# Layer norm of the next batch applied by VectorE instead of GpSimd, in a fused attention and feed-forward kernel

## The reference

```
def _layernorm(x, axis=-1, eps=1e-05):
    m = jnp.mean(x, axis=axis, keepdims=True)
    v = jnp.var(x, axis=axis, keepdims=True)
    return (x - m) / jnp.sqrt(v + eps)
...
    x = L0_attn_x
    xn = _layernorm(x, axis=-1)
    s = _L0_attn_ref(xn, L0_attn_W_attn, L0_attn_b_attn, L0_attn_W_proj, L0_attn_b_proj)
    g = _silu(_L0_ffn_ref(xn, L0_ffn_w_gate, L0_ffn_w_up, L0_ffn_w_down))
    x = x + s * g
    return x
```

## Time and profile before

| | |
|---|---|
| median of 3 runs | 1255.55 us (1254.56 to 1260.43) |
| profiled execution, its span | 1257.5 us |
| PE busy | 1197.4 us, 95% |
| DVE busy | 1013.0 us, 81% |
| ACT busy | 935.2 us, 74% |
| POOL busy | 693.3 us, 55% |
| granted TensorE clock, mean | 0.990 |
| one steady batch | 146.20 us |

### The profile page before, as it was taken

How to read it: one execution, slowest core, us unless ns; L and a number is a source line. 1 busy time by engine, 2 the same in 40 slices (tenths; PEclk the granted TensorE clock), 3 DMA queues, 4 the chain that set the end, 5 groups by cost and what they waited for, 6 DMA issues and landing times.

```text
span 1257.5 us, 29932 instructions
## 1 busy us (share of the span) xinstructions
PE 1197.4 (95%) x11324; PEld 558.3 (44%) x11324; DVE 1013.0 (81%) x2098; ACT 935.2 (74%) x1736; POOL 693.3 (55%) x863
## 2 busy tenths in 40 slices
PE   3889999999999999999999999999999999999986
PEld 2334444545345443544445453454445444454433
DVE  6678988888888888888888888888888888878732
ACT  4447777787877878778777878778787787778774
POOL 4527544395535937177453946369371874446472
PEclk9879999999999999999999999999999999999999
DMA  6140020401222120400204011221204002120101
GB/s 170 47 136 2 2 86 19 119 19 60 53 72 74 35 88 32 119 19 27 85 31 115 20 63 48 86 66 30 91 28 119 19 27 86 39 73 29 42 2 51
DMA packets 56004, 73.23 MB, mean 58 GB/s; under 512 B 8398, under 2 KB 34452, under 8 KB 55860
## 3 DMA queue, kind: packets, MB, share of 16 engines
q1 hardware_dynamic: 55848, 71.30, 18.9%
q10 hardware_dynamic: 12, 0.01, 0.0%
HBM read 44.96 MB, written 25.17 MB: 56 GB/s over the span
## 4 chain that ended last, share of the span: by engine, by line
PE 74%; POOL 10%; DVE 6%; issue 4%; ACT 4%; SPq 1%; DMA 1%; POOLq 0%; DVEq 0%; ACTq 0%
PE ring L854 31%; PE acc L845 17%; PE st L781 11%; PE ring L809 8%; PE ring L927 2%; DVE mx_a L1218 2%; POOL hf L1542 2%; PE ring L824 2%; ACT pexp L1055 2%; POOL hT L1551 1%; PE ring L864 1%; POOL xn L535 1%; PE ring L963 1%; POOL pexp L1512 1%; PE ring L942 1%
## 5 line engine op out<-in xcount | busy, mean ns | idle before, releaser
L1055 ACT ACTIVATE pexp<-st 128x512 f32<-128x512 f32 x1152 | 623.8, 598 | 124.0 <-PE st L781 123.3
L1218 DVE TENSOR_REDUCE mx_a<-ring 128x1 f32<-128x512 f32 (+2 forms) x960 | 536.8, 611 | 50.9 <-PE ring L809 26.0
L1512 POOL TENSOR_SCALAR_AFFINE_SELECT pexp<-pexp 128x512 f32<-128x512 f32 x256 | 158.4, 638 | 412.9 <-ACT pexp L1055 412.9
L845 PE MATMUL acc<-pexp,v_pad 128*17 128x512 f32 (+3 forms) x3072 | 303.7, 490 | 5.8 <-POOL pexp L1512 4.5
L809 PE MATMUL ring<-k_st,q_st 56*128 56x512 f16 (+4 forms) x1536 | 231.4, 326 | 13.3 <-POOL k_st L1641 3.4
L781 PE MATMUL st<-q_st,k_st 58*128 58x512 f16 (+3 forms) x1536 | 231.9, 331 | 6.1 <-ACT pexp L1055 3.4
L1218 DVE TENSOR_REDUCE mx_b<-ring 128x1 f32<-128x384 f32 (+2 forms) x448 | 210.4, 528 | 25.5 <-PE ring L824 24.7
L781 PEld LDWEIGHTS st<-q_st,k_st 58*128 58x128 f16 x1536 | 61.3, 93 | 265.2 <-ACT pexp L1055 173.4
L1542 POOL TENSOR_TENSOR hf<-ga,ups 128x512 f32<-128x512 f32 x96 | 122.4, 1275 | 42.0 <-issue 41.5
L845 PEld LDWEIGHTS acc<-pexp,v_pad 128*17 128x17 f32 x3072 | 61.9, 96 | 129.1 <-issue 105.7
L1551 POOL TENSOR_TENSOR hT<-hf,hT 128x512 f16<-128x512 f32 x96 | 111.4, 1161 | 3.4
(11 more groups left out here) (152 smaller groups left out, 1536.2 us busy)
## 6 DMA issues: line engine op xcount, KB each, us to landing
parts_scratch<-parts SPq DMA_DIRECT2D x32, 512.0 KB, 2.8
q_st<-parts_scratch SPq DMA_DIRECT2D x186, 64.0 KB, 2.2
k_st<-parts_scratch SPq DMA_DIRECT2D x186, 64.0 KB, 2.2
xo<-in_x SPq DMA_DIRECT2D x32, 256.0 KB, 2.9
out<-xo SPq DMA_DIRECT2D x32, 256.0 KB, 2.2
xn<-in_x SPq DMA_DIRECT2D x7, 1024.0 KB, 6.1
q_st<-mT SPq DMA_DIRECT2D x126, 4.0 KB
xn<-in_x SPq DMA_DIRECT2D x2, 512.0 KB, 6.2
```

The source lines that it names most:

```text
L845: mm = nc.tensor.matmul(acc[32 * j:32 * j + D + 1, CH - w:CH], v_pad[:, kb, GH * g + j, :], pexp[:, GH * (m % NSET) + j, at:at + w], start ...
L1055: nc.scalar.activation(pexp[:, GH * (n % NSET) + j, :], st[:, (GH * n + j) % NST, :], ACT.Exp, scale=1.0 / (QK_SCALE * np.sqrt(D))).then_i ...
L1218: top_ = nc.vector.reduce_max(dst, src, AX.X)
L1512: nc.gpsimd.affine_select(out=t, in_=t, compare_op=ALU.is_ge, fill=0.0, base=0, pattern=[[0, GH], [1, P]], channel_multiplier=-1).then_inc ...
```

## The change

LNA moves from GpSimd's list to VectorE's, with the same lag of one half slot and in the same slots. VectorE does it behind the maxima (and, in a half that has them, `split_maxima`) of the second half of slots 8 and 11 to 15, in the same order of tiles. The wait for the finished root, the pause (`stand`) and the instruction are the same. All else stays: the statistics on VectorE, the root on GpSimd, `xn_ready`, TX.

```
 LAG = {
...
-    "vector": {"TX": 0, "QK": 0, "UPG": 0, "DN": 0, "FT": 0, "YT": 0, "LNS": 1, "BP": 0},
-    "gpsimd": {"LNR": 0, "LNA": 1, "XC": 1, "UPU": 2, "HI": 3, "LO": 4, "FP": 2, "FP_G": 3, "FP_X": 4},
+    "vector": {"TX": 0, "QK": 0, "UPG": 0, "DN": 0, "FT": 0, "YT": 0, "LNS": 1, "BP": 0, "LNA": 1},
+    "gpsimd": {"LNR": 0, "XC": 1, "UPU": 2, "HI": 3, "LO": 4, "FP": 2, "FP_G": 3, "FP_X": 4},
...
                 if t[0] == "LNS":
                     return stats(kind, i, t[1])
+                if t[0] == "LNA":
+
+                    dve.wait_ge(ln_chain, LN_EACH * (ln_number(kind, i) + 1))
+                    stand(dve, dve_stand)
+                    return normalise(nc.vector, t[1])
...
                 if t[0] == "LNR":
                     rstd_steps(nc.gpsimd, kind, i, pool_stand)
-                if t[0] == "LNA":
-
-                    pool.wait_ge(ln_chain, LN_EACH * (ln_number(kind, i) + 1))
-                    stand(pool, pool_stand)
-                    normalise(nc.gpsimd, t[1])
```

## The result

| | before | after |
|---|---|---|
| median of 4 runs | 1257.32 us | 1285.97 us (1284.54 to 1287.27) |
| ratio | | 1.023, 95% interval 1.0205 to 1.0255 |
| profiled span | 1257.5 us | 1285.5 us |
| period of a batch, from the issues of the loads of x | 146.2 us | 150.1 us |

The change costs 2.3%, 28 us of span, 4 us a batch on average over seven. The prediction was 1.7% slower, 1276.5 us, in a range from 1254 to 1297. Executions of one kernel differ by some 5 us (the four of before run from 1254.56 to 1260.43), so that a median of few can move by 2 us: it was 1255.55 with three of them.

What follows compares the result with a forecast made beforehand. TensorE, busy 144.87 of 146.20 us a batch, was taken as the bound. Slot losses 1.63 + 0.35 + 0.97 = 2.95, say 3.0 us a batch, 21 us in seven, gave 1276.5 us, range 1254 to 1297.

Steps and rivals of the forecast that it cites:

- the ring: Four banks that VectorE's work frees and TensorE fills next; real slack at 409.89 taken as 0.15 us.
- The wait of 0.67 us: TensorE waits for GpSimd's causal mask at 417.43, once a batch; removing it wins 4.7 us at the most.
- The price of a step: Single step on VectorE 0.62 us, partly held by GpSimd; pair 2.45 at slot 8, 1.5 at slot 15.
- the one row at 1162.55: VectorE's small step on the maxima, a 0.19 us instruction, took 1.21 us, held by a GpSimd tensor_tensor.
- Slot 8: Two steps make VectorE 2.45 us late and TensorE 2.30; without the 0.67 wait, net loss 1.63 us a batch.
- Slot 15: Pair taken as 1.5 us, less idle 0.28 and slack 0.25: loss 0.97 us a batch.
- The uncounted term: VectorE's small steps on the maxima at 431 can be held too, up to 1.2 us each; not counted.
- Slots 11 to 15: Single steps before slot 15's pair: slot 12 loses 0.35 us, slot 11 nothing, slots 13 and 14 nothing or 0.2.
- No hold: Rival: VectorE pays only 0.29 to 0.41 us a step, 1255 to 1258 us; chance 0.16.
- Held to the full: Rival: every step pays 1.57 us, 8.2 us a batch, 1313 us; chance 0.11 for beyond 1297.

Runs made afterwards that it cites:

- relief_ts: relief with GpSimd's five two-input instructions replaced by the tensor_scalar form of its layer norm step; ratio 0.9963 to the kernel before, -4.6 us.
- split2: Kernel before, with GpSimd's two slot 8 steps moved to slots 12 and 14, and those of slots 11 and 13 to VectorE; ratio 0.9993, -0.9 us.
- dve_imm: Changed kernel with constants 0 and 1 in place of mean and root in VectorE's steps; ratio 1.0101 to the kernel before, +12.7 us.
- relief: Kernel before with GpSimd's eight layer norm steps each cut to one column, nothing on VectorE; ratio 1.0036, +4.5 us.
- dve_tiny: Changed kernel with VectorE's layer norm steps cut to one column; ratio 1.0035 to the kernel before, +4.4 us.
- after_ts: Changed kernel with GpSimd's five two-input instructions replaced by the tensor_scalar form of the layer norm step; ratio 1.0009 to the kernel before, +1.1 us.
- singles: Kernel before with only the four steps of slots 11 to 14 on VectorE, slots 8 and 15 left on GpSimd; ratio 1.0031, +3.9 us.

## Why the prediction was right, and where its sizes were off

- **What bounds the kernel.** Right. TensorE is full, and the ring between VectorE and TensorE is tight, but not as tight as read. At the second matmul of slot 9's maxima TensorE is 1.57 us late (409.89, now 419.28, less 7.82), behind a pair of steps that took 2.08. So the slack there was 0.5 us, not 0.15: the row of four maxima from 406.93 is 2.71 us long, where two take 1.29 and four without a break 2.5, so some 0.2 us of idle time of VectorE are hidden in it. I had 2.30 behind a pair of 2.45.
- **What GpSimd gives back.** The wait of 0.67 us is gone in the changed kernel, as forecast, under a larger loss in the same slot. That it is worth 4.7 us by itself fits relief_ts (-4.6), with the reserve above, and split2's steady batches.
- **The price of a step.** The direction was right, by the one row at 1162.55. Its parts were off. The undisturbed step takes 0.40 us, not the 0.29 of the row on b_pr: that row has constants as operands, and dve_imm shows that this is the difference. A held step does not pay its own time after the hold, as I had added it: it ends 0.15 us after GpSimd's instruction. And I counted products and casts only, where masks hold too. The mean in the kernel is 0.797, where I had (2.45 + 4 x 0.62 + 1.5) / 8 = 0.80. The singles are near (0.58 in the steady batch); the pairs are off in opposite directions (2.08 for 2.45, 2.19 for 1.5), so that the equality is luck.
- **Slot 8:** 0.84 us net for 1.63. The pair took 2.08 us, not 2.45: the second step did not come behind the cast with its full time, but ended 0.15 us after it. The rest of the miss is the slack, 0.5 for 0.15.
- **Slot 15:** 2.08 us for 0.97. This is the mis-sized term. I took 1.5 us for the pair, a middle between two bounds, since I couldn't read GpSimd's phase; it took 2.19, which is 0.69 of the miss. The other 0.42 is the slack of 0.53 that I took off: 0.11 was left, since the delays of the slots before had used up VectorE's idle stretch. The pair met two output instructions of 1.27 us one after the other:

```profile
443.16 1.27 POOL L1562 TENSOR_TENSOR so<-so,b_pr 128x512 f32<-128x512 f32 x1
...
443.73 2.19 DVE L535 TENSOR_SCALAR xn<-xn,lnv,rstd 128x256 f32<-128x256 f32 x2
444.50 1.26 POOL L1568 TENSOR_TENSOR so<-so,g 128x512 f32<-128x512 f32 x1
```

- **The uncounted term.** Slots 11 to 15 cost 0.99 us for 0.35: 0.13 where I had the 0.35, and 0.86 behind the steps on the maxima. These were named in the prediction with their price, up to 1.2 us each, and left at nothing: one of 1.23 us and one of 0.49 in a steady batch. The same term turns GpSimd's relief into a loss in relief and dve_tiny, which I hadn't foreseen.
- **The sum.** 0.84 + 0.99 + 2.08 = 3.91 for 2.95. The pair of slot 15 was 1.11 too small, the slots between 0.64 too small, slot 8 0.79 too large: net 0.96 us a batch, 6.7 in seven, of the 7.0 by which the span (1285.5) exceeds the 1278.5 worked out for it.
- **The rivals.** "No hold" is nearly what after_ts makes: the prediction gave it 1255 to 1258 us, at most 0.2% over 1255.55, and the run is 0.09% slower, though its GpSimd is another. "Held to the full" (1313) did not come: GpSimd has idle stretches, and singles cost 3.9 us.

The rule of the Trainium skill (SBUF — State Buffer, "Who interferes with whom") agrees with the held tensor_scalar rows (1.21, 1.47 us). It doesn't tell apart what after_ts tells apart: by it GpSimd's tensor_scalar should block a two-port instruction as its tensor_tensor does, and beside the replaced instructions of that kernel's steady batch the steps took 0.41 to 0.50 us. The measurement decides.

## What to carry to other kernels

Before a step is moved to another engine, look for rows in which a short instruction of that engine took as long as a long one of its neighbour: one such row (1.21 us for 0.19) announced the 23 us of holds here. Moving work off an engine also changes when the rest of it runs, and what stands beside what; a relief of GpSimd by most of 68 us made this kernel slower until its holds on the neighbour were out of the way. A row that merges several instructions can hide idle time between them, and with it slack. And price each place by itself, with the phase of both engines: here slot 8, whose phase I read, came out at half of its forecast and slot 15, where I took a middle, at twice, so that the sum (3.91 for 2.95) was nearer than these two terms.

## What the runs showed of the hardware

- The hold depends on the instructions of both engines. On VectorE: a norm of 256 columns is held up to 1.47 us, the same instruction on one column never (0.257 to 0.269 in 56), statistics over 256 columns never (0.400 to 0.419), but a tensor_scalar on 32 columns up to 1.21 and a tensor_tensor on 16 columns up to 1.23.
- On GpSimd: tensor_tensor (1.16 to 1.28 us), cast (0.61) and `affine_select` (0.63) hold to their end, and a held norm step ends 0.15 us after them. A tensor_scalar over 256 columns with two operands per partition (1.23 us) holds for 0.25 us at the most in the steady batches looked at: a small step takes 0.22 us for 0.19 beside it, and in after_ts 0.44 for 0.19 and a norm step 0.41 to 0.50 for 0.40.
- The other way round, GpSimd's output product (L1568) of 1.26 us took 1.40 in dve_imm, where VectorE's step had gone first.
- A tensor_scalar of 128x256 fp32 on VectorE takes 0.27 to 0.29 us with constants and 0.40 with two operands per partition. A layer norm step on ScalarE takes 0.61, on GpSimd 1.23.
